# An expert layer and a quantised FFN on one core: h turned by DMA instead of by TensorE, and the fp8 rounding shared out anew

## The reference, cut to what matters

```python
def _L0_xattn_ref(hidden_states, token_ids, Wg, Wu, Wd):      # called with Wg = Wu = Wd = ctx_2048, 4 experts of 512x512
    tid = jnp.clip(token_ids, 0, VOCAB - 1)
    expert_ids = jnp.minimum(tid // tokens_per_expert, E - 1)
    out = jnp.zeros_like(hidden_states)
    for e in range(E):
        g = jax.nn.silu(jnp.einsum('bsd,fd->bsf', hidden_states, Wg[e]))
        u = jnp.einsum('bsd,fd->bsf', hidden_states, Wu[e])
        y = jnp.einsum('bsf,df->bsd', g * u, Wd[e])
        out = jnp.where((expert_ids == e)[..., None], y, out)
    return out

def _quantized_matmul(x, w, scale):
    wq = w.astype(jnp.float8_e4m3fn).astype(x.dtype)
    return jnp.einsum('bsi,io->bso', x, wq) * scale

x = x + jnp.tanh(g_xattn[0]) * _L0_xattn_ref(_layernorm(x), itok, ctx_2048, ctx_2048, ctx_2048)
x = x + jnp.tanh(g_ffn[0]) * _L0_ffn_ref(_layernorm(x), ...)    # silu(gate) * up, then down; 512 -> 1536 -> 512, fp8 weights
```

## Time and profile before

| | |
|---|---|
| median of 3 executions | 401.18 us (400.94 to 401.9) |
| the profiled execution | 401.0 us |
| its span (first to last instruction) | 399.3 us |
| TensorE busy | 378.4 us |
| VectorE busy | 224.1 us |
| ScalarE busy | 185.5 us |
| GpSimd busy | 163.2 us |
| granted TensorE clock | 0.994 of full speed |

### The profile page before, as it was taken

The page is one execution under the profiler, slowest core; times in us unless marked ns, Lnnn a source line. Parts: engine busy times, 40 slices in busy tenths (PEclk is TensorE's granted clock), DMA queues, the critical chain, the costliest instruction groups (busy, mean ns, idle before and its releaser), DMA issues.

```text
span 399.3 us, 6082 instructions
## 1 busy us (share of the span) xinstructions
PE 378.4 (95%) x1920; PEld 184.3 (46%) x1920; DVE 224.1 (56%) x467; ACT 185.5 (46%) x297; POOL 163.2 (41%) x204
## 2 busy tenths in 40 slices
PE   3889899999999999999999999999999999999992
PEld 2444455555545544444444444444444444444460
DVE  5878979998787696787434222224222225322253
ACT  3779457789778428693432222222222222222220
POOL 4778889999999831411008000006200004400003
PEclk9999999999999999999999999999999999999997
DMA  7698684354445340760002000001100000200002
GB/s 263 190 313 183 127 214 113 88 108 114 101 115 112 80 105 2 178 167 0 0 2 79 28 0 0 2 0 54 53 0 0 0 0 28 79 0 2 0 0 105
DMA packets 40075, 29.99 MB, mean 75 GB/s; under 512 B 31192, under 2 KB 31216, under 8 KB 40048
## 3 DMA queue, kind: packets, MB, share of 16 engines
q1 hardware_dynamic: 37488, 21.26, 21.4%
q0 software_dynamic: 2560, 8.39, 6.1%
HBM read 18.11 MB, written 4.19 MB: 56 GB/s over the span
## 4 chain that ended last, share of the span: by engine, by line
PE 79%; DVE 10%; ACT 3%; issue 3%; POOL 2%; DMA 1%; SPq 1%; DVEq 0%; ACTq 0%; POOLq 0%
PE bank L1551 36%; PE bank L1565 17%; PE bank L1467 11%; PE bank L1483 7%; PE bank L1391 3%; PE bank L1487 3%; PE bank L1425 1%; DMA X<-x2rows 1%; DVE xs L1112 1%; DVE stats L1062 1%; DVE W L1278 1%; DVE xs L1372 1%; DVE row_hot L997 1%; DVE X L1369 1%; DVE cs L1289 1%
## 5 line engine op out<-in xcount | busy, mean ns | idle before, releaser
L1551 PE MATMUL bank<-X,W 128*128 (+1 forms) x752 | 170.0, 379 | 0.1
L1551 PEld LDWEIGHTS bank<-X,W 128*128 128x128 bf16 x752 | 73.5, 98 | 88.8 <-ACT late_norms L879 0.6
L1289 DVE SCALAR_TENSOR_TENSOR cs<-bank,up_mul,cs 128x512 f32<-128x512 f32 x47 | 35.3, 751 | 107.1 <-PE bank L1551 102.4
L1565 PE MATMUL bank<-W,cs 128*128 128x512 bf16 x376 | 89.0, 379 | 0.5 <-ACT W L762 0.5
L837 ACT ACTIVATE cs<-bank,gate_mul 128x512 f32<-128x512 f32 x47 | 32.2, 684 | 75.5 <-PE bank L1551 75.5
L844 ACT ACTIVATE cs<-cs 128x512 f16<-128x512 f32 x47 | 29.5, 628 | 79.8 <-DVE cs L1289 79.7
L676 POOL TENSOR_TENSOR xs<-xs,X 128x512 f32<-128x512 f32 x12 | 15.3, 1275 | 125.2 <-DVE X L1369 124.9
L1565 PEld LDWEIGHTS bank<-W,cs 128*128 128x128 f16 x376 | 36.6, 98 | 44.0 <-issue 0.5
L1467 PE MATMUL bank<-M,X 128*128 (+1 forms) x228 | 52.5, 379 | 2.1 <-ACT X L728 1.5
L1315 DVE TENSOR_TENSOR cs<-cs 128x512 f16<-128x512 f32 x47 | 33.7, 716 | 31.4 <-ACT cs L844 31.4
L1483 PE MATMUL bank<-M,hTh 128*128 (+1 forms) x152 | 35.9, 378 | 1.6 <-DVE xs L1112 1.6
(11 more groups left out here) (172 smaller groups left out, 385.6 us busy)
## 6 DMA issues: line engine op xcount, KB each, us to landing
ws<-in_L_ffn_gate_w SPq DMA_DIRECT2D x12, 256.0 KB, 2.6
ws<-in_L_ffn_up_w SPq DMA_DIRECT2D x12, 256.0 KB, 3.2
ws<-in_L_ffn_down_w SPq DMA_DIRECT2D x12, 256.0 KB, 2.9
cs<-in_ctx SPq DMA_DIRECT2D x2, 1024.0 KB, 6.7
X<-in_ctx SPq DMA_DIRECT2D x2, 1024.0 KB
xs<-in_x,order POOLq DMA_INDIRECT x16, 4.2
dsc<-in_L_ffn_down_scale SPq DMA_DIRECT2D x1, 256.0 KB
X<-x2rows SPq DMA_TRANSPOSE x16, 3.1
```

Of the source, the lines that this page charges most:

```text
L1289: v.scalar_tensor_tensor(out=fuse[:, c % 2, :], in0=UP[c % 2][:], scalar=up_mul[:, c:c + 1], in1=sg[:, c % 2, :], op0=ALU.mult, op1=ALU.mu ...
L1551: ins = t_.matmul(dst[c % 2][:].rearrange("p (t i) -> p t i", t=TPG), w, x2_group(g, part, k), start=(k == 0 and part == 0), stop=(k == KC ...
L1565: ins = t_.matmul(ACC[t][:], fuse_part(g, c, part)[:, t * P:(t + 1) * P], W8[:, down_slab(c), :], start=(c == 0 and part == 0), stop=(c == ...
```

## The change

**h.** For steps 4 to 18, h is no longer turned by TensorE into a bank and split there. ScalarE makes its high part straight from `h`, VectorE the low part (`h` minus the high part), both as rows of tokens in `hrows`, and SP turns both parts with one transposing DMA into `hT`. `product_y` waits for that DMA (`hT_in`). Steps 0 to 3 are as before.

**Slabs.** 17 slabs are rounded in the steps (two in steps 8 and 12). Of the 19 late ones GpSimd rounds eight (`LATE_POOL`) with `round_late`, for which VectorE does `slab_big`; VectorE rounds eleven with its two instructions. The late slabs come in units of 4, 3, 3, 3, 2, 2, 2.

**Order.** In steps 2 and 3 `product_y` stands ahead of `turn_h`, and the scales of the last expert are made behind `add_expert(0)`. TensorE loads the three words of the step table one by one, in steps 0, 3 and 4. The last `product_y` and `add_expert` stand behind unit 1 of the FFN.

```diff
-    EARLY = 21
-    EARLY_NORMS = 18
-    TURNS = {25: 11, 27: 12, 29: 13, 31: 14, 33: 15}
+    EARLY = 17
+    EARLY_NORMS = 16
+    LATE_UNITS = (("g0", "d1", "g1", "d2"), ("g2", "d3", "g3"), ("g4", "d4", "g5"), ("g6", "d5", "g7"), ("d6", "d7"),
+                  ("d8", "d9"), ("d10", "d11"))
+    LATE_POOL = ("d1", "d2", "d3", "d4", "d5", "d7", "d9", "d11")
+    TURNS = {21: 11, 24: 12, 27: 13, 30: 14, 33: 15}
+    H_DMA = 4
...
-            return 0 if lo < 2 or lo >= STEPS - 1 else 2 if lo in (7, 9, 12, 14, 16) else 1
+            return 0 if lo < 2 or lo >= STEPS - 2 else 2 if lo in (8, 12) else 1
...
+            def turn_h(s):
+
+                sp.wait_ge(y_done, s - 1)
+                sp.wait_ge(hlo_done, s + 1)
+                sp.dma_start_transpose(hT[:, s % 2].rearrange("p a k i -> p (a k) i"),
+                                       hrows[:, s % 2, :]).then_inc(hT_in[s % 2], 16)
...
             for s in range(STEPS):
+                if s > H_DMA:
+                    turn_h(s - 1)
+                if s == STEPS - 1:
+                    turn_h(s)
                 if s >= X2_LAG:
                     turn_x2(s - X2_LAG)
-                for n in slabs_of(s, s):
+                for n in slabs_of(s - 1, s - 1) if s >= 1 else ():
...
+            def round_late(name):
+
+                n = EARLY + LATE_ORDER.index(name)
+                pool.wait_ge(big_done, EARLY + pool_turn(n))
+                row = ws[:, slab_slot(n)]
+                g.tensor_tensor(row, row, w_big[:, slab_slot(n)], ALU.add).then_inc(late_s, 1)
+                pool.wait_ge(late_s, pool_turn(n))
+                g.tensor_tensor(W8[:, n, :], row, w_big[:, slab_slot(n)], ALU.subtract).then_inc(late_q, 1)
...
+                    a.activation(hrows[:, lo % 2, 0:D], h[:], ACT.Copy).then_inc(hhi_done, 1)
...
             def h_low(s, lo):
                 dve.wait_ge(hhi_done, s + 1)
-                v.tensor_tensor(hTl[:, lo % 2, :], HT[:], hTh[:, lo % 2, :], ALU.subtract).then_inc(hlo_done, 1)
+                if lo < H_DMA:
+                    v.tensor_tensor(hT[:, lo % 2, 1], HT[:].rearrange("p (k i) -> p k i", k=KC), hT[:, lo % 2, 0],
+                                    ALU.subtract).then_inc(hlo_done, 1)
+                else:
+                    v.tensor_tensor(hrows[:, lo % 2, D:2 * D], h[:], hrows[:, lo % 2, 0:D],
+                                    ALU.subtract).then_inc(hlo_done, 1)
...
             def group(g, first, last):
                 for c in range(2, IC - 1 if last else IC):
                     unit_fuse(g, c)
                     if first:
-                        late_sum(EARLY + 2 * c - 2)
+                        late_big(late_slabs(c - 1))
+                        late_own(late_slabs(c - 1)[:1])
                     unit_low(g, c)
                     if first:
-                        late_round(EARLY + 2 * c - 2)
-                        late_sum(EARLY + 2 * c - 1)
-                        late_round(EARLY + 2 * c - 1)
+                        late_own(late_slabs(c - 1)[1:])
...
-                if lo >= 1:
-                    turn_h(s - 1, lo - 1)
+                if 1 <= lo <= H_DMA:
+                    turn_h(s - 1, lo - 1)
...
+                else:
+                    pe.wait_ge(hT_in[lo % 2], h_turns(lo))
...
             gate_or_up(0, 0, 1)
+            gate_up(0, 1)
             product_y(STEPS - 1, STEPS - 1)
-            gate_up(0, 1)
             gate_up(0, 2)
             down(0, 0)
```

More of the change, by code:

```diff
@@ L361, in down_slab, with late_slabs, by_pool, pool_turn @@
             return EARLY_NORMS + c if EARLY_NORMS + c < EARLY else EARLY + LATE_ORDER.index(f"d{c}")
+        def late_slabs(c):
+            first = EARLY + sum(len(unit) for unit in LATE_UNITS[:c])
+            return range(first, first + len(LATE_UNITS[c])) if c < len(LATE_UNITS) else ()
+        def by_pool(n):
+            return n >= EARLY and LATE_ORDER[n - EARLY] in LATE_POOL
+        def pool_turn(n):
+            return sum(by_pool(m) for m in range(n + 1))
+        def own_turn(n):
+            return n + 1 - pool_turn(n)
+        def slab_summed(engine, n):
+            if by_pool(n):
+                engine.wait_ge(late_q, pool_turn(n))
+            else:
+                engine.wait_ge(sum_done, own_turn(n))
+        def slab_rounded(engine, n):
+            if by_pool(n):
+                engine.wait_ge(late_q, pool_turn(n))
+            else:
+                engine.wait_ge(q_done, own_turn(n))
         def walk_words(engine):
@@ L665, in _ @@
             x2_low(TILES - 5)
-            for i in range(3):
-                ln_scalars(STEPS + STATS1_LEAD + i, (STEPS + i) % 2, 1, 2)
-            for i in range(4):
-                x2_low(TILES - 4 + i)
+            round_late("d1")
+            ln_scalars(STEPS + STATS1_LEAD, STEPS % 2, 1, 2)
+            round_late("d2")
+            ln_scalars(STEPS + STATS1_LEAD + 1, (STEPS + 1) % 2, 1, 2)
+            x2_low(TILES - 4)
+            round_late("d3")
+            ln_scalars(STEPS + STATS1_LEAD + 2, STEPS % 2, 1, 2)
+            x2_low(TILES - 3)
+            round_late("d4")
+            x2_low(TILES - 2)
+            round_late("d5")
+            x2_low(TILES - 1)
+            round_late("d7")
+            round_late("d9")
             ffn_norm(1, 2 * KC, IC)
+            round_late("d11")
             for t in range(TILES):
@@ L895, in group @@
                     gate_silu(g, c)
-                    if first and 5 <= c < 8:
+                    if first and 4 <= c < 8:
                         late_norm(c)
@@ L1228, in step @@
                     x1_low(s + 1)
-                if lo >= 2 and lo != 3:
+                if lo in (2, 4):
                     h_low(s - 1, lo - 1)
@@ L1232, in step @@
                     norms_in()
+                    h_low(s, lo)
                     add_expert(s - 2)
@@ L1246, in step @@
                     round_stats(s, lo)
+                if H_DMA <= lo < STEPS - 1:
+                    h_low(s, lo)
                 for n in slabs_of(s, lo):
@@ L1331, in _ @@
             unit_low(0, 1)
+            add_expert(STEPS - 1)
             def group(g, first, last):
@@ L1427, in _ @@
             pe.wait_ge(order_done, 1)
+            words = walk_words(pe)
+            load_word(t_, words, 0)
             pe.wait_ge(xn_done, 1)
@@ L1516, in step @@
                               stop=True).then_inc(msum_done, 1)
+                if lo in (2, 3):
+                    product_y(s - 2, lo - 2)
+                if 1 <= lo <= H_DMA:
+                    turn_h(s - 1, lo - 1)
+                for n in squared_of(s - 1, lo - 1) if lo >= 1 else ():
+                    norms(n, n, n % 2, SMALL, KC * n)
+                if lo in (3, 4):
+                    load_word(t_, words, lo - 2)
+                if lo < STEPS - 1:
+                    z_next[0] = z_operands(s + 1, lo + 1)
                 if lo >= 4:
@@ L1528, in norms @@
                 ins.then_inc(norm_done, 1)
-            for i in range(WORDS):
-                load_word(t_, words, i)
             z_next = [z_operands(0, 0)]
```

125 lines of the change are left out of this document (68 added, 57 removed).

## The result

| | before | after |
|---|---|---|
| median of the runs, us | 401.5 (400.9 to 402.2, 4 runs) | 412.4 (409.6, 409.8, 414.9, 414.9) |
| ratio after to before, 95% interval | | 1.027 [1.017, 1.036] |
| profiled execution, its span, granted clock | 401.0, 399.3, 0.994 | 414.9, 413.1, 0.977 |

The change makes the kernel 2.7% slower (1.7 to 3.6% by the interval). The forecast was 398.2 us with a range up to 404.5. The four runs fall in two pairs 5 us apart and the profiled one is of the slower pair, so marks read from its trace hold some us that the median doesn't, and a difference of under about 3 us to the median of 412.4 says little.

What follows compares the result with a forecast made beforehand. TensorE, busy for 378.4 of 399.3 us, was taken as the bound. The terms, 401.0 - 5.7 + 1.6 - 1.2 + 2.4, gave 398.1 us for the profiled execution, 398.2 beside the median; range 393.9 to 404.5.

Steps and rivals of the forecast that it cites:

- 1, the turns: Between z(5) and z(18), 13 turns of h leave TensorE: -5.7 us.
- 2, doubled steps: In steps 8 and 12, with two slabs, late GpSimd blocks VectorE: +1.2 and +0.4, sum +1.6 us.
- 3, early steps: add_expert goes ahead of the last expert's scales, so h(2) comes earlier and TensorE's early waits shrink: -1.2 us.
- 5, SP and the DMA: In the steps, h's DMA lands at 8.5 us, y(s) begins at 12.0; 3.4 us cover it: 0.
- The rival of the late DMA: In the steps, SP waits for GpSimd's x2_low, h's DMA comes late and y waits: 406 us, chance 0.07.
- 4, the late stage: From z(18) to down(0, 6), VectorE's list plus GpSimd's blocking makes 51.3 us instead of 48.9: +2.4.
- b: VectorE time lost per GpSimd instruction, taken as 0.53 us; the late stretch is 43.4 + 15 b while VectorE is last.
- the gain is eaten exactly: Rival: b from 0.64 to 0.80 gives 399.8 to 402.2 us, chance 0.15.
- the rival in which VectorE and GpSimd take turns: Units 0 to 5 of group 0: nearly every instruction collides; 403.0 us at b = 0.85, 407.6 at 1.15; chance 0.30.
- The x2_low at 165 and 171 did not collide: Argument against the second rival, from the kernel before: two late GpSimd instructions did not block VectorE.
- the signs that the prediction named: Right: TensorE waits 2 to 4 us at down(0, 0). Wrong: 2 us or more at down(0, 3) and down(0, 4).
- The range of the likeliest case: Whole kernel: b between 0.3 and 0.64 gives about 395.8 to 399.8 us, chance 0.33.

Runs made afterwards that it cites:

- e14: Changed kernel, h in PSUM and by DMA from step 6, x2 turned later, early and late orders undone, VectorE rounding late slabs, two ahead of unit 0: 397.9 us.
- e17: e14 with h turned by TensorE in all steps; 401.8 us, 1.000 of the kernel before.
- e4: Changed kernel with h turned by DMA from step 8 on instead of step 4; 410.9 us, 1.023 of the kernel before.
- e3: Changed kernel with all 19 late slabs rounded by VectorE and none by GpSimd; 409.4 us, 1.017 of the kernel before.
- e15: e14 with four slabs ahead of unit 0, as in the changed kernel; 403.7 us, 1.004 of the kernel before.
- e16: e14 with GpSimd rounding the same eight late slabs as in the changed kernel; 408.3 us, 1.015 of the kernel before.

## Why the prediction was wrong

The profiled execution came out at 414.9, 16.8 us above the sum of 398.1. Its steps, in their order:

- **1, the turns (-5.7).** Right in size: undisturbed steps are 5.72 us, from step 15 on 5.28. With nothing late, 12 turns taken out of the steps (e14 against e17) gave 3.9 us of their 5.3.
- **2, doubled steps (+1.6).** VectorE's own price was about 0.6 (one wait for add_expert at 88.28, in step 10). The mechanism was right (slab_big took 1.50 us at 85.98 and 112.72, h_low 1.65 at 92.0, 118.6 and 123.5, behind both doubled steps), but the stall that counts was missed: GpSimd's lateness in a doubled step passes by SP to the DMA.
- **3, early steps (-1.2).** The waits for add_expert went; the one for h(3) grew from 1.3 to 2.4 us, and in the profiled run the clock fell behind it: +1.2 instead of -1.2. Without the lower clock (e4) silu(5) is at 52.4, as before: the edit gives 0. I had let the gain of one wait pass down the chain without following h(3). (The rows are step 11, as the prediction says, and not 12, as their heading has it.)
- **5, SP and the DMA (0).** This is the step that failed. I laid the lists of a single-slab step side by side, found 3.4 us of cover, and took a landing time of 3.1 us from the turns of x2, which are issued ahead of their step's loads. At y(9) and y(13) (waits of 1.8 and 1.2 us) GpSimd's lateness in the doubled step held SP (ahead of the DMA for y(9) x2_low ended 6.3 us behind the start of h, a step earlier 2.7), and two loads then stood ahead of the DMA. At y(4) (3.4 us) it was neither GpSimd nor SP: the row came 8.8 us behind z(4) and not 4.7, and the landing took 7.5 and not 3.1. It cost 6.4 us of waits, and 3.6 of lower clock behind them, for which the sum had no term. The rival of the late DMA named the mechanism of y(9) and y(13), not that of y(4), and had 0.07.
- To z(18), against the forecast: +2.4 early, +6.4 waits, +3.6 clock, -1.0 of term 2, which makes 11.4; the marks say 11.1.
- **4, the late stage (+2.4).** down(0, 0) was forecast at 21.7 behind z(18) and came at 22.4. down(0, 6) came at 56.9 instead of 51.3. In the form of the forecast, 43.4 + 15b, that is b = 0.90 and not 0.53. But 1.7 us of it is again the clock (24 matmuls from 181.66 on), which leaves b = 0.79, at the upper end of the rival "the gain is eaten exactly". The picture in the rows is that of the rival in which VectorE and GpSimd take turns, which had 0.30 of the chance. From 138 to 200 us 14 of VectorE's 30 instructions with two 128x512 inputs in SBUF were long, and 15 of GpSimd's 20 took 1.6 to 1.75 us instead of 1.15 to 1.3. "The x2_low at 165 and 171 did not collide" was the wrong comparison: in this stretch GpSimd was busy for 16 of 49 us before and for 36 of 57 after. b is not the whole either: without GpSimd's roundings (e3) the stretch is still 54.0, 1.7 of it the clock (16 matmuls of down in 5.3 instead of 3.6), and the four slabs ahead of unit 0, whose price the forecast took from the list, cost 5.8 us by themselves (e15 against e14). Of the signs that the prediction named, the wait of 2 to 4 us at down(0, 0) came (3.6); those at down(0, 3) and down(0, 4), which were to tell the second rival, were 1.0 and 1.2 us and not 2 or more, so they would have missed it.
- **The range of the likeliest case** was wrong at its low end. At b = 0.3 TensorE is last behind down(0, 0): 20.8 + 23.5 + 5.4 = 49.7, so +0.8 and 396.5 us, not 395.8.

The choice of b as an average over six instructions, some of which met an idle VectorE, and the cover of 3.4 us taken from the typical step instead of the worst one, are the two errors. Two of the rivals came true together, and the range did not add one to the other.

What stays open: why the clock falls behind one wait and not behind another as long, why h(4) lands after 4.9 us in one run and 7.5 in another, why 12 turns less give 3.9 us and not 5.3, and how much of GpSimd's 10.4 us in e16 (against 3.0 in e3) is due to the tighter list there.
